# Cross-attention and routed experts on one core: the first group ahead of the second at the start, the last tile's row statistics ahead of the experts' low parts at the end

## The reference

```python
# cross-attention: 16 heads of 32, queries from layernorm(x), keys and values from ctx_1024
q, k, v = layernorm(x) @ Wq.T, ctx @ Wk.T, ctx @ Wv.T          # split into heads
scores = q . k / sqrt(32);  masked where padding or attention mask is False
x = x + softmax(scores) @ v @ Wo.T                             # fully masked rows give 0
# routed experts: the expert of a position depends on the position alone
idx = argmax(pe(position) . sign(tile_sigs))                   # 8 experts
x = x + (layernorm(x) @ W[idx].T + b[idx])
```

## Time and profile before

| | us |
|---|---|
| median of three runs (lowest, highest) | 964.98 (964.84, 965.28) |
| the profiled execution, its own time | 966.44 |
| its span, first to last instruction | 964.5 |
| TensorE busy in the span | 908.4 (94%) |
| VectorE, GpSimd, ScalarE busy | 734.6, 571.2, 384.0 |
| granted TensorE clock, mean | 0.979 of full |
| mean of `y_rstd`'s three operations (L996, L997, L999) | 0.25, 0.25, 0.60 |

### The profile page before, as it was taken

The page is one execution under the profiler, slowest core; times in us unless marked ns, Lnnn a source line. Parts: engine busy times, 40 slices in busy tenths (PEclk is TensorE's granted clock), DMA queues, the critical chain, the costliest instruction groups (busy, mean ns, idle before and its releaser), DMA issues.

```text
span 964.5 us, 16646 instructions
## 1 busy us (share of the span) xinstructions
PE 908.4 (94%) x5696; PEld 729.2 (76%) x5697; DVE 734.6 (76%) x1097; ACT 384.0 (40%) x697; POOL 571.2 (59%) x764
## 2 busy tenths in 40 slices
PE   5889999999999999999999999999718999999997
PEld 3668878878878878878878878887516888888885
DVE  5788777687787678788677787779766777777775
ACT  5355444444544445444444545444532111111110
POOL 4346557464654745556464655744675777777773
PEclk9899999999999999999999999999977999999999
DMA  9423131331313223131331313114624445545551
GB/s 339 155 108 112 55 101 56 111 100 55 112 45 113 65 90 112 56 100 56 111 91 60 116 45 112 56 45 134 227 83 126 151 163 163 163 156 162 164 164 48
DMA packets 48876, 108.10 MB, mean 112 GB/s; under 512 B 10496, under 2 KB 15136, under 8 KB 46624
## 3 DMA queue, kind: packets, MB, share of 16 engines
q1 hardware_dynamic: 36928, 71.39, 23.2%
q0 software_dynamic: 11200, 35.21, 11.4%
q10 hardware_dynamic: 672, 0.52, 0.2%
HBM read 73.47 MB, written 35.19 MB: 113 GB/s over the span
## 4 chain that ended last, share of the span: by engine, by line
PE 90%; POOL 2%; DVE 2%; DMA 2%; ACT 1%; issue 1%; SPq 1%; DVEq 0%; ACTq 0%; POOLq 0%
PE pS L1356 28%; PE pA L1645 21%; PE pA L1356 19%; PE pS L1414 7%; PE pA L1437 7%; PE pT L1425 5%; PE pT L1625 3%; DMA xt_raw<-in_x_t 1%; PE pS L1382 1%; DMA wf_hl<-in_wf 1%; POOL xt_lo L980 1%; POOL wf_hl L303 0%; POOL y L996 0%; SPq L913 0%; DVE row L1204 0%
## 5 line engine op out<-in xcount | busy, mean ns | idle before, releaser
L1645 PE MATMUL pA<-wf_hl,x_hi 128*128 x560 | 183.0, 408 | 0.0
L1199 DVE TENSOR_TENSOR s<-pS,bias 128x1024 f32<-128x1024 f32 x64 | 78.2, 1222 | 106.8 <-PE pS L1414 105.2
L996 POOL COPY y<-y_mom 128x1 f32<-128x1 f32 x64 | 16.1, 251 | 238.8 <-DVE y_mom L1238 238.8
L1013 POOL TENSOR_TENSOR s<-s,row 128x1024 f32<-128x1024 f32 x64 | 121.9, 1905 | 16.3 <-DVE row L1219 16.3
L1543 POOL DMA_INDIRECT out_dram<-y,scatter_rows x70 | 94.8, 1355 | 54.3 <-DVE y L1591 54.3
L1115 ACT CAST ot_hi<-pA 128x512 fp32r<-128x512 f32 x64 | 37.6, 588 | 224.2 <-PE pA L1437 224.2
L1645 PEld LDWEIGHTS pA<-wf_hl,x_hi 128*128 128x128 f32 x560 | 100.9, 190 | 19.2 <-issue 0.3
L1562 ACT CAST x_hi<-pT 128x512 fp32r<-128x512 f32 x70 | 41.1, 587 | 186.1 <-PE pT L1625 152.6
L1356 PE MATMUL pA<-wo_hi,ot_hi 128*128 128x512 f32 x256 | 108.8, 425 | 4.5 <-DVE ot_lo L1223 4.5
L1645 PE MATMUL pA<-wf_hl,x_lo 128*128 x280 | 111.2, 397 | 0.0
L980 POOL TENSOR_TENSOR xt_lo<-xt_raw,xt_hi 128x512 fp32r<-128x512 f32 x64 | 95.1, 1520 | 21.1 <-ACT xt_hi L1071 21.1
(11 more groups left out here) (124 smaller groups left out, 1907.3 us busy)
## 6 DMA issues: line engine op xcount, KB each, us to landing
x_scratch<-y SPq DMA_DIRECT2D x64, 257.0 KB, 3.0
xt_raw<-in_x_t SPq DMA_DIRECT2D x16, 1024.0 KB, 6.1
x<-in_x SPq DMA_DIRECT2D x64, 256.0 KB, 2.6
wf_hl<-in_wf SPq DMA_DIRECT2D x8, 1024.0 KB, 8.8
ctx_raw<-in_ctx_t SPq DMA_DIRECT2D x32, 128.0 KB, 3.1
bias_all<-in_bf SPq DMA_DIRECT2D x1, 2048.0 KB, 9.7
mask_early<-in_mask SPq DMA_DIRECT2D x1, 1536.0 KB, 13.6
xg<-x_scratch,gather_rows POOLq DMA_INDIRECT x70, 3.5
```

The lines of the kernel that those rows point to most:

```text
L1013: pool.tensor_tensor(p, p, h.row[:, t % h.c, 3, :].unsqueeze(2).broadcast_to([P, H, BK]), ALU.mult)\
L1199: dve.tensor_tensor(h.s_sb[:, t % h.c, :].rearrange("p (h k) -> p h k", h=H), pS[:, 0, :].rearrange("p (h k) -> p h k", h=H), h.bias[:, t ...
L1645: mm = pe.matmul(pA[:, r % 2, :], a[:, c * P:(c + 1) * P], w, start=(c == 0 and m == 0), stop=(c == KC - 1 and m == 2))
```

## The change

At the start, TensorE's list takes the first group through K, Q and the scores before the second group's K and the first group's V; `transpose_k(0)` now stands ahead of the column sums of Q's weight, and K ahead of the routing's first product. ScalarE's copies follow that order: `xt_high(1)`, `k_copy(1)` and `ctx_high(1)` move behind the first group's work, `exps(0)` ahead of `v_copy(0)`, and `exps(1)` behind the first `pt_copy`, inside the loop. VectorE takes its routing steps and the mask test ahead of `moments` and V's low part; O's low part goes to GpSimd. SyncE loads `x_t` of the first group ahead of Q's weight, and takes over two small table loads from ScalarE's queue.

At the end, expert 1's low part is split between GpSimd and VectorE; after the last tile's moments VectorE waits for `y_ready` to reach 64 before expert 2's low part, and the low parts of 4, 5, 6 and 7 move into the experts' part of its list. ScalarE's high parts of experts 0 and 2 move by about one tile. SyncE issues expert 3's load ahead of the last tile's store.

```diff
@@ SyncE, start
             for c in range(KC):
                 load_w(wk_raw, wk, wk_loaded[c], c)
+            load_xt(0)
             for c in range(KC):
                 load_w(wq_raw, wq, wq_loaded[c], c)
-            load_xt(0)
             load_ctx(1)
...
+            sp.dma_start(slots[:], slots_d).then_inc(slots_loaded, 16)
+            sp.dma_start(place[:], place_d).then_inc(slots_loaded, 16)
@@ SyncE, end
                 store_y(h.tiles - 2)
-                store_y(h.tiles - 1)
                 sp.wait_ge(op_done, h.tiles)
                 load_expert_set(sp, LAST_FREE)
+                store_y(h.tiles - 1)
@@ GpSimd, start and end
             rstd(1)
+            pool.wait_ge(w_hi_ready["o"], 1)
+            pool.tensor_tensor(w_lo["o"][:].rearrange("p c n -> p (c n)"), wo_raw[:],
+                               w_hi["o"][:].rearrange("p c n -> p (c n)").bitcast(F32), ALU.subtract)\
+                .then_inc(w_lo_ready["o"], 1)
             xt_low(1)
...
-                expert_low(pool, 1, 1, 1)
+                expert_low(pool, 1, 1, 1).then_inc(wf_lo_pool, 1)
                 y_rstd(h.tiles - 2)
-                expert_low(pool, 1, 2, 2)
-                expert_low(pool, 1, 3, 3).then_inc(wf_lo_pool, 1)
                 y_rstd(h.tiles - 1)
@@ ScalarE, in the loop
                     pt_copy(t)
+                    if t == 0:
+                        exps(1)
+                    if t == h.tiles - 2:
+                        expert_high(act, 0)
+                    if t == h.tiles - 1:
+                        expert_high(act, 2)
@@ VectorE, start
             for c in range(KC):
                 low_part("q", wq_raw, c)
-            moments(0)
-            moments(1)
...
-            low("v", wv_raw)
+            dve.wait_ge(mask_loaded, 16)
+            dve.tensor_reduce(early[:], mask_early[:]..., AX.X, ALU.max).then_inc(early_max, 1)
+            moments(0)
+            moments(1)
...
-            low("o", wo_raw)
+            low("v", wv_raw)
@@ VectorE, end of the loop and experts
-                expert_low(dve, 2).then_inc(wf_lo_dve, 1)
+                expert_low(dve, 1, 2, 3).then_inc(wf_lo_dve, 1)
                 residual(h.tiles - 1)
                 y_moments(h.tiles - 1)
-                for t in (4, 5, 6, 7):
-                    expert_low(dve, t).then_inc(wf_lo_dve, 1)
+                dve.wait_ge(y_ready, h.tiles)
+                expert_low(dve, 2).then_inc(wf_lo_dve, 1)
...
+            expert_low(dve, 4)
+            expert_low(dve, 5)
             normalise(0)
+            normalise(1)
+            expert_low(dve, 6)
             low(0)
-            normalise(1)
             add_bias(0)
...
                 if j == 0:
+                    expert_low(dve, 7)
                     expert_low(dve, 3).then_inc(wf_lo_ready, NE - 3)
@@ TensorE, start
+            project_k(0)
+
             pe.wait_ge(rv, 3)
...
-            project_k(0)
+            transpose_k(0)
...
-            transpose_k(0)
...
-            project_k(1)
             for m in range(KC):
                 project_q(0, m)
-            pe.wait_ge(early_max, 1)
-            pe.matmul(pA[0:1, 1, 300:301], early[:], ones[:, 0:1], start=True, stop=True).then_inc(early_sum, 1)
-            scores(0)
-            project_v(0)
...
+            pe.wait_ge(early_max, 1)
+            pe.matmul(pA[0:1, 1, 300:301], early[:], ones[:, 0:1], start=True, stop=True).then_inc(early_sum, 1)
+            scores(0)
+            project_k(1)
+            project_v(0)
             scores(1)
```

More of the change, by code:

```diff
@@ L524, in full_gpsimd @@
                 group(i)
-            for t in (0, 1):
-                expert_low(pool, t).then_inc(wf_lo_pool, 1)
+            expert_low(pool, 0).then_inc(wf_lo_pool, 1)
+            expert_low(pool, 1, 0, 1).then_inc(wf_lo_pool, 1)
         def full_scalar(act, f):
@@ L729, in full_vector @@
                 group(i)
-            for t in (2, 4, 5, 6, 7):
-                expert_low(dve, t).then_inc(wf_lo_dve, 1)
+            expert_low(dve, 1, 2, 3).then_inc(wf_lo_dve, 1)
+            expert_low(dve, 2).then_inc(wf_lo_dve, 1)
         def full_tensor(pe, f):
@@ L1140, in short_scalar @@
             q_copy(0, 0)
-            q_copy(0, 1)
             act.wait_ge(wo_loaded, 16)
             act.copy(w_hi["o"][:].rearrange("p c n -> p (c n)"), wo_raw[:]).then_inc(w_hi_ready["o"], 1)
+            q_copy(0, 1)
             q_copy(0, 2)
+            q_copy(0, 3)
             xt_high(1)
-            q_copy(0, 3)
+            k_copy(1)
+            exps(0)
             v_copy(0)
-            exps(0)
             kt_copy(1)
-            exps(1)
             q_copy(1, 0)
@@ L1175, in tiles @@
                         q_copy(g + 2, 0)
-                    if t == h.tiles - 3:
-                        expert_high(act, 0)
                     if t == h.tiles - 2:
                         expert_high(act, 1)
-                        expert_high(act, 2)
                 for t in (4, 5, 6, 7, 3):
@@ L1268, in short_vector @@
             dve.memset(h.vd[:, 1], 0.0).then_inc(zeroed, 1)
+            for c in range(2):
+                low_part("k", wk_raw, c)
             dve.wait_ge(chosen_loaded, 48)
@@ L1272, in short_vector @@
             done(dve.tensor_tensor(sgn[:, 2, :], sgn[:, 0, :], sgn[:, 1, :], ALU.subtract))
-            for c in range(KC):
+            for c in range(2, KC):
                 low_part("k", wk_raw, c)
@@ L1308, in short_vector @@
             done(dve.tensor_tensor(match[:, :, 1, :], match[:, :, 0, :], halves_wide(c_pos, PB * NR), ALU.mult))
-            low("v", wv_raw)
+            dve.wait_ge(mask_loaded, 16)
+            dve.tensor_reduce(early[:], mask_early[:].rearrange("p k n -> p (k n)").bitcast(U32), AX.X, ALU.max)\
+                .then_inc(early_max, 1)
+            moments(0)
+            moments(1)
             done(dve.tensor_tensor(expert_f[:], c_block[0:1, :].unsqueeze(2).broadcast_to([1, NR, NE - 1]),
@@ L1368, in project_k @@
                 pe.wait_ge(ctx_lo_ready, g + 1)
-                dst = free_bank(0, 1 if g == 1 else 3 * g)
+                dst = free_bank(0, 3 * g)
                 for k in range(KC):
@@ L1377, in transpose_k @@
                 dst = free_bank(1, 4 * g)
-                pe.wait_ge(q_drained[0], 2 if g == 1 else 3 * g + 1)
+                pe.wait_ge(q_drained[0], 3 * g + 1)
                 if g == 0:
```

19 lines of the change are left out of this document (7 added, 12 removed).

## The result

The changed kernel took **953.64 us** (median of 4 runs, 952.88 to 954.80), the kernel before 965.13 (4 runs): a ratio of 0.988, 95% interval 0.9863 to 0.9897. It is faster, by 11.5 us, inside the range of 945 to 954.5 and 4.1 us above the forecast of 949.5. The forecast's own narrower range, 948 to 951.5, was missed. The profiled executions are 13.1 us apart, 966.44 and 953.35.

A forecast was written before the change was run, and what follows sets the result against it. The tile loop was taken as bound by TensorE and untouched; start 9.0 plus end 6.5 gave 15.5 us off the profiled 966.44, 950.9, and with the median 1.46 lower, 949.5 us. Own range 948 to 951.5, eight in ten 945 to 954.5.

The forecast's parts named there:

- GpSimd getting in first: Rival at the start: O's low part issued before V's, so V(0) waits; start gains 5.1, time 953.4 us; 15%.
- later gathers held: Rival at the end: later gathers also held, two low parts delay several blocks; end gives 4, time 952 us; 9%.
- Q of the first group at 20.8, scores(0) at 34.5: Start: Q begins at 20.8 instead of 28.27 us, the first scores at about 34.5 instead of 42.38.
- VectorE's low part first, then GpSimd's until 40.1, the third step held until 41.3: Start: V's low part ends about 35 us, O's runs to 40.1, holding mask_scores(0)'s 1.23 us third step until 41.3.
- Q of group 1 from 45.2 to 48.0: Into the loop: Q waits for GpSimd's xt_lo until 45.1, runs 45.2 to 48.0; first weigh_v at 50.1 us.
- that sign of being wrong (over 3 us): Sign against the start's forecast: TensorE idle for more than 3 us before K(1)'s transposes.
- The loop is untouched: Tile loop: bound by TensorE, whose products the change leaves alone, so no TensorE idle time between 60 and 600 us.
- both rivals that lost the gain there: Loop: late loads, start gains 2 to 3, 956 us, 5%; or 0.3 us waiting per tile, 967.6 us, 3%.
- `y_ready` 9.9 us sooner: End: last tile's moments 0.4 us sooner, small GpSimd steps take 1.1 us; y_ready at 706.7 instead of 716.58.
- The store 5.0 us ahead of the first gather: End: last store queues behind expert 3's 1 MB, so the first gather starts between 710.9 and 712.3; taken as 711.7.
- The first gather held by a low part until 713.7: End: VectorE's low parts hold the gather to 713.7, so normalise(0) runs at 717.3, or 715.4 if not held.
- 9.0 us from the first product to block 3: End: VectorE's list takes 9.0 us instead of 7.6, TensorE waits 1.4 for normalise(3); block 3's transposes at 731.0.

The follow-up runs named there:

- r5: The changed kernel itself, unaltered, run once more as a measure of how much its start varies: 954.44 us, ratio 0.9883.
- r1: The changed kernel with the last tile's store issued ahead of expert 3's load: 951.65 us, ratio 0.985.
- r2: The changed kernel's start only, with the end of the kernel before: 962.00 us, ratio 0.9952.
- r4: The changed kernel with expert 6's low part ahead of VectorE's first normalise: 952.35 us, ratio 0.9855.
- r10: The changed kernel with products that nothing reads put in TensorE's idle time at the start and before the experts: 951.03 us, ratio 0.9856.
- r7: The changed kernel with the edits of r6 and r1 together: 951.90 us, ratio 0.9856.
- r8: r7 with the low parts of experts 4 and 5 in four pieces each and expert 6's behind low(0): 954.34 us, ratio 0.9886.
- r12: r10's filling, with 28 products instead of 34 after the last y_rstd, and r1's store order: 948.59 us, ratio 0.9827.
- r6: The changed kernel with O's low part on GpSimd moved behind xt_low(1): 954.28 us, ratio 0.9883.

## Why the prediction was right or wrong

The start was forecast as 9.0 and measured as 7.8 in this profile, 6.1 to 6.6 in four others; the end as 6.5 and measured as 5.3 (13.11 less 7.78). That is 2.4 us of the miss in the profiled execution. The other 1.75 are the step from one execution to the median: I took it 1.46 below, and it lies 0.29 above. All three erred the same way, and the time stayed inside the wide range by 0.9 us (r5, the same kernel again, by 0.06); its upper end was there for two rivals, GpSimd getting in first and later gathers held, whose start of 5.1 and end of 4 were not what happened. So the mechanisms held and the sizes did not, and that the number lies inside is partly luck.

- *Q of the first group at 20.8, scores(0) at 34.5:* 19.86 and 33.37. Right, a little sooner, and the half-clock stretch that I had put there came: granted 0.50 from 21 to 24, and 13.5 us from the one to the other where I had 13.7. In r5, r1 and r2 Q's first product is at 21.12, 20.96 and 21.09, as K's products began later or took longer, and in r1, r4 and r5 no stretch stands there, and a longer one does from K(1)'s transposes on.
- *VectorE's low part first, then GpSimd's until 40.1, the third step held until 41.3:* 32.10, 39.06 and 40.15. Right, the turns and their price. The rival in which GpSimd gets in first did not happen, but it was near. GpSimd's last `rstd` step was held by V's low part for 1.9 us; with its usual 0.29 it would have been through at 32.6, 0.5 us behind the start of V's low part, which is the distance I had counted.
- *Q of group 1 from 45.2 to 48.0:* it started at 44.99 and ended at 49.20. **This is the term that was mis-sized:** I had put a half-clock stretch at Q of the first group and none here, although my own numbers had TensorE idle from 42.4 to 44.0 and again just before 45.2. It costs 1.4 us here, and with the idle time filled it is gone (r10). In r1, r4 and r5 TensorE waits 3.0 us ahead of K(1)'s transposes and the lower clock lasts longer there, though V's low part ended ahead of O's: that sign of being wrong (over 3 us) was just reached in r5, by another way than the rival's.
- *The loop is untouched:* 612.35 us from tile 1 to tile 61 in both. Right; the loads behind the flag arrived in time, and both rivals that lost the gain there are out. Two figures of the second are wrong as they stand: at 0.3 us in each of 62 tiles its time is 949.5 + 18.6 = 968.1, not 967.6; and 8.9 us is the shorter kind of tile (from tile 1 to tile 2), where the mean of the loop is 10.2 (612.35 over 60).
- *`y_ready` 9.9 us sooner:* 16.55 less 7.78 is 8.8. The small steps took their 1.1 us, as forecast (9.4 us gained there), but the second-to-last tile took 0.9 back, at the lower clock (0.50 from 680 to 685); the last returned 0.2.
- *The store 5.0 us ahead of the first gather:* 7.20. The second mis-sized term, 2.2 us. I had asked whether the megabyte "still moves" and taken the middle; it was issued 2.7 us ahead and the store was behind all of it. r1 shows it: 3.99 us and 2.1 us sooner at block 3.
- *The first gather held by a low part until 713.7:* not here, since the late store let the low parts end first, 0.14 us before the gather. The mechanism is right (r1, r4: 1.97 and 2.86 us). By the forecast's clock the gather came at 715.0: two errors that nearly met.
- *9.0 us from the first product to block 3:* 8.25, with 0.07 us of waiting instead of 1.4: at the lower clock TensorE's own products take nearly as long as the list. The list is right: with the store first, `normalise(3)` ends 22.2 to 22.5 us behind `y_ready` in r1, r7, r8 and r12, in each 0.1 to 0.2 us ahead of the mark.

## What to carry to other kernels

Where a wait of TensorE is moved and not removed, count what follows it at the lower clock (1.4 us for 12 products here), and take that from more than one profile: five of the same start were 1.7 us apart. A small store that someone waits for goes into a queue ahead of a large load that nobody waits for yet (3 us at the gather here for two lines changed places, and 2 to 2.5 of the time). Before an operation is given to another engine, ask whom its whole length holds there: 2048 columns on GpSimd held VectorE in both places where they stood, for 2.99 us at a step of 1.23 and for 3.20 and 4.52 at steps of 0.2.

## What the runs showed of the hardware

- An indirect gather of GpSimd, 0.95 to 1.24 us alone, took 1.97 and 2.86 beside a VectorE subtraction with two SBUF inputs, and ended 0.8 to 1.1 us behind it.
- Beside a two-input operation of GpSimd, VectorE's `tensor_reduce` of 1024 columns took its usual 1.22 us, and a `tensor_scalar` of 16 columns 3.20 instead of 0.17 (r6): the length of the operation does not decide. The Trainium skill ("SBUF — State Buffer", "Who interferes with whom") says that on this chip `tensor_reduce` never contends and that `tensor_scalar` can, under conditions on its operands. The trace agrees with both.
- With 28 to 34 products in the wait before the experts, the granted clock of the whole span rose to 0.992 from 0.981, but only the filling at the start is shown to buy time.
